# First Gram matrix corrected behind both splits of the second ctx, instead of between them

## Chip, cores and metric

One Trainium2 chip, one of its cores. The metric is the device time of one launch in microseconds (us), the median of several runs.

## The reference, cut to what is computed

Eight batches; x and ctx of a batch are 256 channels (rows) by 1024 columns, all in 32-bit floats.

```python
# cross attention, for each batch b (B=8, C=256, D=1024, 8 groups of 32 channels)
t = Wt @ ctx          # (256, 1024)
p = Wp @ layernorm(x)
g = Wg @ ctx
...
att = sum over a group of (p * g)          # one number per group
y = Wz (per group) @ (att * t)
yn = (y - mean) * rsqrt(var + 1e-5)        # over a group
x = x + tanh(g_xattn) * (yn * gn_w + gn_b + ctx)
# feed-forward with 64 experts of rank 8, for each row
h = layernorm(x); scores = (h Wq^T) keys^T; gate = softmax over the top 16 of 64
x = x + tanh(g_ffn) * 2 * ((h A^T) * gate) B^T
```

## The kernel before, in words

**Tiling.** 256 channels are T = 2 tiles of 128 rows, 1024 columns are NH = 2 halves of 512. A loop over the NB = 8 batches is written out by hand, one program for each engine: SP (SyncE) issues the loads and stores, PE (TensorE) multiplies, DVE (VectorE), ACT (ScalarE) and POOL (GpSimd) work on the elements. Each engine takes its instructions strictly in the order of its program, and each waits on counting semaphores that other engines raise. No scheduler is at work: what stands earlier in the text of an engine's block runs earlier.

**Attention by a Gram matrix.** att needs only M = (normed x) ctx^T, 256 x 256. `whole_gram(0)` (L1104) multiplies the raw x by ctx into two PSUM banks, z_ps[0] and z_ps[1], one for each tile of 128 rows. As x is not yet normed there, `gram_fix(n)` on DVE (L787) subtracts from bank t the row means times the column sums of ctx (`cb_sb`): one instruction of 128 x 256 for each t, which waits for `gram_done` of its bank and raises `M_fixed`. `M_high(n)` on ACT (L545) waits for `M_fixed`, scales by the reciprocal deviation and writes M_first (which lies in zg_sb) for batch 0; it raises `M_hi_s`. `first_n()` on PE (L1198) waits for both and multiplies by Wp. `att_reduce(0)` (L817) on DVE multiplies its result by Wg and sums.

**The group statistics.** `group_means(n)` (L1223, PE) averages the means of u over groups of 32 rows, `group_deviation(n)` (L823, DVE) waits for it (`mean_sum`) and raises `mean_read`, for which `u_variance(n)` (L538, ACT) waits; `group_att_var(0)` (L1229, PE) needs the result.

**Splits in two parts.** The products of u = Wu ctx are done in three passes with each operand split in a high and a low part. Of the second ctx (batch 1), `c_high(t, 1)` on ACT (L520) writes c_hi, and `second_c_low(t)` on DVE (L956) writes c_lo = c_sb - c_hi, 128 x 1024, both operands and the result in SBUF. It waits for c_hi of the tile, for the last u product of batch 0 and for the first low part, and raises `c_lo_s`. `u_product(1)` on PE (L1185) waits for both tiles of c_lo.

**Around it.** On POOL, `x_add(0)` (L418) adds x to ctx of batch 0, four instructions of 128 x 512, all in SBUF. PE's program in this stretch is `ctx_sums(0)`, `whole_gram(0)`, `group_means(0)`, 8 small products for the router (L1342, 64 columns each), `first_n()`, `u_product(1, {0: group_att_var(0)})`, then the transposes `hT(0, 0)` (L1243) of w and the products `z_product(0, 0)` (L1266). ACT's is `c_high(0, 1)`, `c_high(1, 1)`, `u_copy(0)` (L557, four), `M_high(0)`, `u_variance(0)`, the router's high part (L636), then the high parts of twelve lots of weights (L616), then `hT_high(0, 0)` (L574). DVE's goes on with the router's low part (L981), `att_reduce(0)`, and `slopes(0, two_lots)` (L833 to L847), with the low parts of two lots (L744) in it while POOL takes a root (`y_root`, L428); then `first_w` (L855). The four pieces of `first_w` need `xt_done` of `x_add(0)`.

Of the kernel before, what the change touches and what calls it, by code (L numbers as in the profile page):

```python
# [6 lines left out]
def flamingo_block(nc, x, ctx, xT, cT, wt, wzT, wpT, wg, aT, bT, wq, keysT, norms, out):  # L7
# [27 lines left out]
    with ExitStack() as stack:  # L35
# [87 lines left out]
        def gram_bank(n, t):  # L123
            return w_ps[T + t] if n == 2 else z_ps[t]
# [50 lines left out]
        def per_tile(n, t):  # L175
            return T * n + t + 1
# [9 lines left out]
        def per_use(n, k):  # L186
            return USES * n + k + 1
# [543 lines left out]
        def _(dve):  # L731
# [6 lines left out]
            def settle():  # L738
                dve.wait_ge(dve_step, steps[0])
# [41 lines left out]
            def gram_fix(n):  # L781

                dve.wait_ge(cb_s, n + 1)
                settle()
                for t in range(T):
                    dve.wait_ge(gram_done, per_tile(n, t))
                    dve.scalar_tensor_tensor(gram_bank(n, t)[:, 0:C], cb_sb[:, :], neg_x[:, t:t + 1], gram_bank(n, t)[:, 0:C],  # L787
                                             ALU.mult, ALU.add).then_inc(M_fixed, 1)
# [7 lines left out]
            def u_statistics(n, tiles=range(T)):  # L796
                for t in u_tiles(n):
                    if t not in tiles:
                        continue
                    for h in range(NH):  # L800
                        k = NH * t + h
                        dve.wait_ge(u_done, per_use(0, first_uses().index(k)) if n == 0 else u_use(n, k))
                        step(dve.bn_stats(u_st[:, t, 6 * h:6 * h + 6], w_ps[k][:, :]))  # L803
                    settle()
                    instruction = dve.bn_aggr(u_mv[:, t, :], u_st[:, t, :])
                    instruction.then_inc(u_stats, 1)
                    dve.wait_ge(u_stats, u_tile(n, t))
                    dve.tensor_scalar(neg_u[:, t:t + 1], u_mv[:, t, 0:1], -1.0, None, ALU.mult).then_inc(u_mean, 1)  # L808
# [12 lines left out]
            def group_deviation(n):  # L821
                dve.wait_ge(mean_sum, n + 1)
                dve.tensor_tensor(u_dev[:, :], u_mv[:, :, 0], t_ps[1][:, 0:T], ALU.subtract).then_inc(mean_read, 1)  # L823
                if n >= 2:

                    dve.wait_ge(mean_read, n + 1)
                    step(dve.tensor_tensor(a2[:, :], u_dev[:, :], u_dev[:, :], ALU.mult))
                    settle()
                    dve.tensor_tensor(att_var[:, T:2 * T], a2[:, :], u_mv[:, :, 1], ALU.add).then_inc(u_rows, T)
# [122 lines left out]
            def second_c_low(t):  # L952
                dve.wait_ge(c_hi_s, per_tile(1, t))
                dve.wait_ge(u_done, per_use(0, USES - 1))
                dve.wait_ge(first_lo_s, t + 1)
                dve.tensor_tensor(c_lo[:, t, :], c_sb[1][:, t, :], c_hi[:, t, :].bitcast(f32),  # L956
                                  ALU.subtract).then_inc(c_lo_s, 1)
# [16 lines left out]
            minus_means(0)  # L974
            u_statistics(0)
            second_c_low(0)
            gram_fix(0)
            group_deviation(0)
            second_c_low(1)
            dve.wait_ge(router_hi_s, 1)  # L980
            dve.tensor_tensor(A_lo[:, :, NN:ZC], t_ps[0][:, :].rearrange("p (k e) -> p k e", k=KD),  # L981
                              A_hi[:, :, NN:ZC].bitcast(f32), ALU.subtract).then_inc(router_lo_s, 1)
# [476 lines left out]
```

## Time and profile before

| | us |
|---|---|
| median of 3 runs | 324.51 |
| lowest, highest | 324.15, 326.56 |
| the profiled execution | 325.73 |
| its span, first to last instruction | 323.9 |
| PE busy in the span | 319.0 (98%) |
| DVE, ACT, POOL busy | 245.9, 174.9, 168.5 |

The page shows the profiled execution: busy time of each engine, the span in 40 slices with the granted clock of TensorE, the chain of work that ended last, and the costliest groups of instructions. A timeline row gives start, duration, engine, line and operation, with the tensors written and read. Where several instructions are merged (x4), the duration is from the first's start to the last's end. Successive instructions of one engine overlap in the records by some hundredths of a microsecond, since one is started before the last one has drained.

### The profile page before, as it was taken

How to read it: one execution, taken by the hardware profiler on the slowest of the kernel's cores; microseconds unless marked ns; L12 is line 12 of the kernel's file. 1: busy time of each engine (PE TensorE's matmuls, PEld its weight loads, DVE VectorE, ACT ScalarE, POOL GpSimd, SP SyncE). 2: the span in 40 equal slices, each digit the busy share in tenths (PEclk: the TensorE clock that was granted, in tenths of full speed). 3: DMA queues.
4: the chain of work that ended last, by engine and by line, in shares of the span. 5: the costliest groups of instructions: out<-in, count | busy, mean ns of one | idle time of the engine just before them, and what ended most of it. 6: DMA issues, size and time to landing. Idle time of an engine off the chain costs nothing.

```text
span 323.9 us, 5543 instructions
## 1 busy us (share of the span) xinstructions
PE 319.0 (98%) x1960; PEld 290.4 (90%) x1960; DVE 245.9 (76%) x636; ACT 174.9 (54%) x298; POOL 168.5 (52%) x158
## 2 busy tenths in 40 slices
PE   8999999999999999999999999999999999999996
PEld 6688998899988999898999899898999889989985
DVE  1856897596588946888887799788987798789362
ACT  3687845677256485286545658177454654354110
POOL 0464699189463969339581677429591580010000
PEclk9998999999999999999999999999999999999999
DMA  7999900990650585249951899228961631272102
GB/s 248 412 388 397 363 4 7 328 306 10 191 200 13 184 300 190 63 134 272 405 200 34 253 358 361 67 89 275 365 252 61 224 134 74 58 244 82 65 32 99
DMA packets 28091, 62.69 MB, mean 194 GB/s; under 512 B 2448, under 2 KB 12560, under 8 KB 28064
## 3 DMA queue, kind: packets, MB, share of 16 engines
q1 hardware_dynamic: 27712, 62.14, 54.6%
q8 instruction: 16, 0.26, 0.3%
q10 hardware_dynamic: 352, 0.20, 0.2%
q14 instruction: 11, 0.09, 0.1%
HBM read 46.34 MB, written 15.99 MB: 192 GB/s over the span
## 4 chain that ended last, share of the span: by engine, by line
PE 94%; DMA 3%; SPq 1%; issue 0%; ACT 0%; DVE 0%
PE z_ps L1266 20%; PE w_ps L1296 18%; PE w_ps L1185 12%; PE w_ps L1266 12%; PE z_ps L1125 9%; PE w_ps L1303 9%; PE z_ps L1104 4%; DMA cT_first<-in_cT 3%; PE t_ps L1213 2%; PE w_ps L1125 2%; PE t_ps L1243 2%; PE t_ps L1280 1%; PE z_ps L1198 1%; PE z_ps L1213 1%; PE t_ps L1342 1%; PE w_ps L1314 0%
## 5 line engine op out<-in xcount | busy, mean ns | idle before, releaser
L1296 PE MATMUL w_ps<-B_hi,zT_hi 128*128 128x512 f32 x124 | 49.3, 397 | 0.0
L1296 PE MATMUL w_ps<-B_lo,zT_hi 128*128 128x512 f32 x124 | 48.4, 391 | 0.0
L384 POOL TENSOR_TENSOR xT_lo<-xT_in,xT_hi 128x512 fp32r<-128x512 f32 x24 | 30.6, 1298 | 20.5 <-ACT xT_hi L500 17.7
L418 POOL TENSOR_TENSOR c_sb<-c_sb,x_sb 128x512 f32<-128x512 f32 x28 | 36.2, 1329 | 6.9 <-ACT c_sb L603 6.9
L403 POOL TENSOR_TENSOR c_lo<-c_sb,c_hi 128x512 fp32r<-128x512 f32 x24 | 30.3, 1292 | 14.1 <-DVE uw L863 14.1
L557 ACT ACTIVATE uw<-w_ps,neg_u 128x512 f32<-128x512 f32 x32 | 20.2, 686 | 28.8 <-DVE neg_u L808 28.8
L574 ACT ACTIVATE hT_hi<-t_ps 128x512 fp32r<-128x512 f32 x32 | 18.5, 599 | 30.7 <-DVE t_ps L884 22.5
L1266 PE MATMUL z_ps<-A_hi,hT_hi 128*128 128x288 f32 x160 | 34.7, 298 | 0.2 <-ACT hT_hi L574 0.2
L1266 PE MATMUL z_ps<-A_lo,hT_hi 128*128 128x288 f32 x160 | 34.1, 294 | 0.0
L1303 PE MATMUL w_ps<-B_hi,zT_lo 128*128 128x512 f32 x124 | 33.3, 390 | 0.0
L384 POOL TENSOR_TENSOR cT_lo<-cT_in,cT_hi 128x512 fp32r<-128x512 f32 x24 | 30.6, 1300 | 2.4 <-DVE uw L863 2.4
L1303 PEld LDWEIGHTS w_ps<-B_hi,zT_lo 128*128 128x128 f32 x124 | 23.3, 188 | 5.0
L1296 PEld LDWEIGHTS w_ps<-B_hi,zT_hi 128*128 128x128 f32 x124 | 23.3, 188 | 4.4
L1296 PEld LDWEIGHTS w_ps<-B_lo,zT_hi 128*128 128x128 f32 x124 | 23.3, 188 | 4.3
L1266 PEld LDWEIGHTS z_ps<-A_hi,hT_hi 128*128 128x128 f32 x160 | 25.9, 188 | 1.1 <-ACT hT_hi L574 0.4
L1266 PEld LDWEIGHTS z_ps<-A_lo,hT_hi 128*128 128x128 f32 x160 | 25.9, 189 | 0.0
L942 DVE SCALAR_TENSOR_TENSOR uw<-w_ps,tg,uw 128x512 f32<-128x512 f32 x31 | 22.5, 743 | 2.9 <-PE w_ps L1303 2.7
L1266 PE MATMUL z_ps<-A_hi,hT_lo 128*128 128x288 f32 x160 | 24.7, 297 | 0.0
L803 DVE BATCH_NORM_STATS2 u_st<-w_ps 128x6 f32<-128x512 f32 x32 | 21.2, 690 | 3.3 <-PE w_ps L1185 3.3
L1125 PE MATMUL z_ps<-cT_hi,xT_hi 128*128 128x256 f32 x80 | 23.7, 296 | 0.0
L870 DVE TENSOR_TENSOR hT_lo<-t_ps,hT_hi 128x512 fp32r<-128x512 f32 x32 | 21.4, 682 | 1.9 <-ACT hT_hi L574 1.0
L1185 PE MATMUL w_ps<-c_hi,Wu_hi 128*128 128x512 f32 x56 | 22.7, 405 | 0.0
(191 smaller groups left out, 846.8 us busy)
## 6 DMA issues: line engine op xcount, KB each, us to landing
c_sb<-in_ctx SPq DMA_DIRECT2D x16, 512.0 KB, 6.8
x_sb<-in_x SPq DMA_DIRECT2D x16, 512.0 KB, 7.3
xT_in<-in_xT SPq DMA_DIRECT2D x14, 512.0 KB, 6.8
cT_in<-in_cT SPq DMA_DIRECT2D x14, 512.0 KB, 8.1
out_block<-uw SPq DMA_DIRECT2D x14, 512.0 KB, 6.2
w_through<-uw SPq DMA_DIRECT2D x10, 512.0 KB, 3.2
c_sb<-w_through SPq DMA_DIRECT2D x10, 512.0 KB, 4.0
z_through<-zg_sb SPq DMA_DIRECT2D x9, 256.0 KB, 2.3
```

The source lines that it names most:

```text
L384: last = pool.tensor_tensor(lo[:, chunks, :], came[:, chunks, :], hi[:, chunks, :].bitcast(f32), ALU.subtract)
L403: last = pool.tensor_tensor(c_lo[:, t, cols], c_sb[n % 2][:, t, cols], c_hi[:, t, cols].bitcast(f32), ALU.subtract)
L418: last = pool.tensor_tensor(c_sb[n % 2][:, t, cols], c_sb[n % 2][:, t, cols], x_sb[:, t, cols], ALU.add)
L557: act.activation(uw[n % 2][:, t, cols], w_ps[k][:, :], ACT.Identity, bias=neg_u[:, t:t + 1]).then_inc(u_copied, 1)
L803: step(dve.bn_stats(u_st[:, t, 6 * h:6 * h + 6], w_ps[k][:, :]))
L870: dve.tensor_tensor(hT_lo[at], t_ps[g][:, :], hT_hi[at].bitcast(f32), ALU.subtract).then_inc(hT_lo_s, 1)
L942: dve.scalar_tensor_tensor(uw[n % 2][:, t, cols], w_ps[k][:, :], tg2[:, 0:1], uw[n % 2][:, t, cols], ALU.mult, ALU.add).then_inc(out_added, 1)
L1125: last = pe.matmul(gram_bank(n, t)[:, 0:C], a[:, k, t * P:(t + 1) * P], c[:, k, :], start=(k == 0 and a is xT_hi and c is cT_hi), stop=(k ...
L1185: last = pe.matmul(w_ps[k][:, :], w[:, c, rows], v[:, c, cols], start=(c == 0 and w is Wu_hi and v is c_hi), stop=(c == T - 1 and w is Wu_lo))
L1266: last = pe.matmul(banks[i][:, 0:ZH], (hT_lo if low else hT_hi)[:, t, k * P:k * P + P], w[:, k, i * ZH:(i + 1) * ZH], start=(k == 0 and no ...
L1296: pe.matmul(w_ps[k][:, :], zT_hi[:, t, row], w[:, j, cols], start=(j == 0 and w is B_hi), stop=False)
L1303: last = pe.matmul(w_ps[k][:, :], zT_lo[:, t, j * P:(j + 1) * P], B_hi[:, j, cols], start=False, stop=(j == KN - 1))
```

## The change

In DVE's program for batch 0, the second of the two splits, `second_c_low(1)`, stands directly behind the first, and `gram_fix(0)` and `group_deviation(0)` behind both. Nothing is added or removed, and the waits of each piece are the same as before.

```diff
             minus_means(0)
             u_statistics(0)
             second_c_low(0)
+            second_c_low(1)
             gram_fix(0)
             group_deviation(0)
-            second_c_low(1)
             dve.wait_ge(router_hi_s, 1)
```

DVE's order around the place, as the difference of the two programs (L956 is `second_c_low`, L787 `gram_fix` on the banks z_ps, L823 `group_deviation`, L981 the router's low part):

```order
 L808 TENSOR_SCALAR neg_u<-u_mv 128x1
-L956 TENSOR_TENSOR c_lo<-c_sb,c_hi 128x1024
-L787 SCALAR_TENSOR_TENSOR z_ps<-cb_sb,neg_x,z_ps 128x256 x2
-L823 TENSOR_TENSOR u_dev<-u_mv,t_ps 128x2
-L956 TENSOR_TENSOR c_lo<-c_sb,c_hi 128x1024
+L956 TENSOR_TENSOR c_lo<-c_sb,c_hi 128x1024 x2
+L787 SCALAR_TENSOR_TENSOR z_ps<-cb_sb,neg_x,z_ps 128x256 x2
+L823 TENSOR_TENSOR u_dev<-u_mv,t_ps 128x2
 L981 TENSOR_TENSOR A_lo<-t_ps,A_hi 128x8x64
```

The two corrections and the deviation have moved behind one more instruction of 128 x 1024; what follows L981 stands as it did.

ACT's order at the same place, the same in both programs (L557 the copies of u, L545 `M_high(0)`, L538 `u_variance(0)`, L636 and L616 high parts of weights):

```order
L520 ACTIVATE c_hi,c_sum<-c_sb 128x1024 x2
L557 ACTIVATE uw<-w_ps,neg_u 128x512 x4
L545 ACTIVATE zg_sb<-z_ps,x_rs 128x256 x2
L538 ACTIVATE att_var<-u_dev,u_mv 128x1 x2
L636 ACTIVATE A_hi<-t_ps 128x8x64
L616 ACTIVATE A_hi<-A_in 128x512 x8
```

Nothing moved here; L545 waits for L787 of DVE, L538 for L823, and L636 stands behind both. The programs of PE, POOL and SP are also the same in both kernels.

## Rows read from the trace of the kernel before

**Rows 1.** The page, busy time of TensorE in the span: busy us (share), instructions

```profile
PE 319.0 (98%) x1960; PEld 290.4 (90%) x1960; DVE 245.9 (76%) x636; ACT 174.9 (54%) x298; POOL 168.5 (52%) x158
```

**Rows 2.** Chain that ended last, in order of time: start us, us, what

```profile
15.79 5.42 PE z_ps L1104 x24
```

**Rows 3.** Waits of PE from 16 us to the end: us in total, times, longest

```profile
PE z_ps L1104 <- DMA cT_first<-in_cT: 0.3, 1, 0.3
PE z_ps L1266 <- ACT hT_hi L574: 0.2, 1, 0.2
```

**Rows 4.** Timeline of PE: start us, us, line, operation, tensors

```profile
21.25 1.99 PE L1342 MATMUL t_ps<-stage 16*128 16x64 f32 x16
23.17 2.99 PE L1198 MATMUL z_ps<-zg_sb,Wp_in 128*128 128x256 f32 x8
25.60 0.99 PE L1185 MATMUL w_ps<-c_hi,Wu_hi 128*128 128x512 f32 x1
```

**Rows 5.** Timeline of DVE, 18 to 27 us (in brackets: idle before, and what ended it)

```profile
18.22 2.02 DVE L956 TENSOR_TENSOR c_lo<-c_sb,c_hi 128x1024 fp32r<-128x1024 f32 x1 [1.88 <-ACT c_hi L520]
20.16 0.47 DVE L787 SCALAR_TENSOR_TENSOR z_ps<-cb_sb,neg_x,z_ps 128x256 f32<-128x256 f32 x1
21.24 0.49 DVE L787 SCALAR_TENSOR_TENSOR z_ps<-cb_sb,neg_x,z_ps 128x256 f32<-128x256 f32 x1 [0.61 <-PE z_ps L1104]
...
21.71 1.22 DVE L956 TENSOR_TENSOR c_lo<-c_sb,c_hi 128x1024 fp32r<-128x1024 f32 x1
23.91 0.69 DVE L981 TENSOR_TENSOR A_lo<-t_ps,A_hi 128x512 fp32r<-128x512 f32 x1 [0.98 <-ACT A_hi L636]
26.31 0.43 DVE L817 CUSTOM_DVE_ANT_0 z_ps<-z_ps,Wg_sb 128x256 f32<-128x256 f32 x1 [1.71 <-PE z_ps L1198]
```

**Rows 6.** Timeline of ACT, 19 to 33 us

```profile
19.28 0.19 ACT L520 ACTIVATION_READ_ACCUMULATOR c_hi<-c_sb 128x1 f32 x1
19.37 2.41 ACT L557 ACTIVATE uw<-w_ps,neg_u 128x512 f32<-128x512 f32 x4
21.66 0.85 ACT L545 ACTIVATE zg_sb<-z_ps,x_rs 128x256 f32<-128x256 f32 x2
22.37 0.69 ACT L538 ACTIVATE att_var<-u_dev,u_mv 128x1 f32<-128x1 f32 x2
23.28 0.60 ACT L636 ACTIVATE A_hi<-t_ps 128x512 fp32r<-128x512 f32 x1 [0.22 <-PE t_ps L1342]
...
32.98 1.09 ACT L574 ACTIVATE hT_hi<-t_ps 128x512 fp32r<-128x512 f32 x2 [2.87 <-PE t_ps L1243]
```

**Rows 7.** Timeline of POOL, third and fourth piece of x_add(0)

```profile
17.88 1.27 POOL L418 TENSOR_TENSOR c_sb<-c_sb,x_sb 128x512 f32<-128x512 f32 x1
19.11 2.25 POOL L418 TENSOR_TENSOR c_sb<-c_sb,x_sb 128x512 f32<-128x512 f32 x1
```

**Rows 8.** Timeline of DVE and POOL where both work in SBUF, 29 and 35 us

```profile
29.06 1.28 DVE L744 TENSOR_TENSOR A_lo<-A_in,A_hi 128x512 fp32r<-128x512 f32 x2
29.22 1.09 POOL L428 TENSOR_TENSOR y_rs<-y_ve,minus_half 128x2 f32<-128x2 f32 x1 [2.23 <-DVE y_ve L841]
...
35.48 1.41 DVE L744 TENSOR_TENSOR A_lo<-A_in,A_hi 128x512 fp32r<-128x512 f32 x1
36.30 1.75 POOL L391 TENSOR_TENSOR A_lo<-A_in,A_hi 128x512 fp32r<-128x512 f32 x1
```

**Rows 9.** All eight of L428: duration ns min/median/max, first and last start

```profile
L428 POOL TENSOR_TENSOR y_rs<-y_ve,minus_half x8: 688/690/1088, 29.2 to 281.4; 128x2 f32<-128x2 f32 x8
```

**Rows 10.** Timeline of DVE and ACT, the same correction and scaling of batch 1

```profile
55.05 0.87 DVE L787 SCALAR_TENSOR_TENSOR z_ps<-cb_sb,neg_x,z_ps 128x256 f32<-128x256 f32 x2
55.62 0.84 ACT L545 ACTIVATE M_hi<-z_ps,x_rs 128x256 fp32r<-128x256 f32 x2 [2.01 <-DVE z_ps L787]
```

**Rows 11.** Windows of PE: A:B, us, busy (x), granted clock, DMA share, GB/s

```profile
24.00:27.40 3.40, 3.40 (x10) 0.50 1.06 395
27.40:32.40 5.00, 5.00 (x25) 1.00 1.04 398
```

## The prediction

> **What bounds the kernel now.** I read the page's busy times first. TensorE is busy for 319.0 of 323.9 us [rows 1], so only something that makes PE wait, run slower or do less can move the end; the other engines count where PE waits for them. Next I read the chain that ended last: from 15.79 us, where the first Gram matrix starts, it lies on PE nearly without a break [rows 2]. The waits of PE say the same: from 16 us to the end it is shown idle twice, 0.3 us for the first transposed inputs and 0.2 us for a high part of the turned w [rows 3]. The change lies behind the first and ahead of the second. It gives PE no work and takes none, so with no stall to remove on PE, a gain could only come from TensorE's clock. The question is whether the later correction makes PE wait, and how long.
>
> PE's row of work there is: 16 small router products, start 21.25; then `first_n`, start 23.17; then `u_product(1)`, start 25.60 [rows 4]. `first_n` needs both tiles of M_high, which need both corrections.
>
> **Slack before the change.** The two corrections start at 20.16 and 21.24, the second only then because its Gram bank was not ready (0.61 us idle), and it ends at 21.73 [rows 5]. ACT scales both tiles in 21.66 to 22.51 [rows 6]. PE comes to `first_n` at 23.17, so M is there 0.66 us early (0.56 with the handover that is worked out below) [rows 4, 6]. The other consumer, `u_product(1)`, has its second low part at 21.71 + 1.22 = 22.93 and starts at 25.60 [rows 4, 5]: 2.67 us of slack. Having that low part sooner brings nothing; that half of the move is worth 0.
>
> **When the second split now ends.** Its inputs are ready: c_hi of tile 1 is complete at 19.28 + 0.19 = 19.47, and the first split hands over to the next instruction at 20.16 [rows 5, 6]. So it is issued at 20.16. How long it takes depends on POOL. The first split took 2.02 us and the second 1.22, at the same shape [rows 5]. Beside the first, POOL's third piece of `x_add` ran 17.88 to 19.15 unstretched, while the fourth, started at 19.11, took 2.25 instead of 1.27 and ended at 21.36 [rows 7]. That reads as one at a time: the split waits from 18.22 to 19.15 and works 1.09 us, until 20.24; the fourth piece waits for it and works 1.12 us behind it. A second place agrees: L744 takes 1.41 us against 0.68 for one of a pair (1.28 for two, which overlap by 0.08), and the POOL instruction that starts at 36.30 behind it takes 1.75 [rows 8]. The Trainium skill, "GPSIMD Engine Reference", Key points, says that GpSimd shares its SBUF interfaces with VectorE and that the two contend when a VectorE instruction has two SBUF inputs. This trace agrees (2.02 against 1.22 us); without that rule the move would look free, as the third case below works out.
>
> Before, the correction stood at 20.16, which has its bank in PSUM and only one large input in SBUF: it took 0.47 us beside POOL, its usual time [rows 5, 7], while the second split at 21.71 came after POOL had finished. Now the second split meets POOL's fourth piece, which has waited since 19.11. Who goes first? The nearest row is the root at 29.22. It came while a pair of L744 ran from 29.06 to 30.34. The root took 1.09 us against a median of 0.69 [rows 8, 9], so it was held 0.40 us, to 29.62, about the end of the first of the pair (29.06 + 0.68 = 29.74), and ended at 30.31, ahead of the pair's end. A POOL instruction that waits thus gets its turn between two back-to-back DVE instructions. I take that: the fourth piece runs to 21.36 as before, then the split works 1.09 us, to 22.45, and hands over 0.08 us before its end, at 22.37. The bounds: DVE keeps its turn (issue 20.16, 1.22 us, handover at 21.30), or the two are interleaved as on average in the first split (2.02 us, handover at 22.10), or POOL's piece goes first (22.37).
>
> **From the split to PE.** Both Gram banks are full by 21.24, so the corrections follow back to back. Batch 1 shows such a chain: corrections start at 55.05, the scaling on ACT starts 0.57 us later and takes 0.84 for both tiles [rows 10], 1.41 from the first correction's start to the last scaling's end. So 22.37 + 1.41 = 23.78. From ACT to PE I add 0.10 us, an estimate from the handover from DVE to ACT (the reader starts 0.57 us behind a correction that takes 0.47 [rows 5, 10]): 23.88. Against 23.17 that is a **stall of 0.71 us on PE**, at a place where it now has none.
>
> **What else is late, and what covers it.** `group_deviation` moves from about 21.7 to 22.37 + 0.87 = about 23.2, and ACT issues `u_variance` behind the scaling at about 23.7 instead of 22.37; it takes 0.69 [rows 6, 10]. The router's high part behind it starts at about 24.35 instead of 23.28, and the twelve lots with it, 1.07 us late. ACT is idle for 2.87 us ahead of 32.98 [rows 6], which covers this. The router's low part on DVE is then at 23.91 + 1.07 = 24.98 to 25.67, ahead of `att_reduce` at 26.31 + 0.71 [rows 5]. POOL takes up the first lots later by the same 1.07 us, and its next root is 0.71 us later too; the two instructions of 1.3 us in front of it have 2.23 us of idle time behind them [rows 8]. So these cost 0. If this cover were gone, the 1.07 us would cost its excess over the stall, 0.36 us. SP's queue and all DMAs stand untouched.
>
> After `first_n`, `att_reduce`, `slopes`, the first w and the turned h hang on its result and shift with PE. The wait of 0.2 us for hT_hi [rows 3] is made by the same chain, so it does not absorb the shift, and no wait for a transfer lies behind it.
>
> **Sum.** 0 (work) + 0.71 (stall) - 0 (low part sooner) = +0.71 us. The profiled execution took 325.73 us, 1.83 more than its span of 323.9, and would be 326.4; it lay 1.22 above the median, 324.51. From the median: 324.51 + 0.71 = **325.2 us**, 0.2% slower. Three runs of this kernel spread by 0.7% (324.15 to 326.56), so within 1%, about 3.2 us, is what a measurement can hardly tell from no change.
>
> **TensorE's clock.** From 24.00 to 27.40 PE was granted 0.50, the 1.2 GHz level, and from 27.40 again 1.00, the 2.4 GHz level [rows 11]. Ahead of the fall PE did the small router products and started `first_n`. The 3.4 us at half speed cost 1.7 us against full speed. The stall falls just ahead of this stretch and adds 0.71 us without products to a time of small products. If the stretch keeps its length, nothing changes. The Trainium skill, "TensorE: Matmul & The Clock Gate", Part 1, says that the clock gate follows how busy the array has lately been. That speaks for a longer slow stretch and not a shorter one; no row here shows by how much.
>
> **The rivals.**
> 1. *PE stalls by POOL's turn, clock as before* (the forecast): +0.71, 325.2 us. Chance 0.48.
> 2. *The stall is smaller.* Interleaved, the handover at 22.10 gives 22.10 + 1.51 = 23.61 and a stall of 0.44: 324.95 us. Speaks for it: the 2.02 us are also what equal shares would give; against it: the third piece at 1.27 was not stretched. Chance 0.12.
> 3. *No stall.* DVE keeps its turn: handover at 21.30, ACT is busy with the copies of u until 21.78 and then scales from 21.87 to 22.71, with the handover 22.81, 0.36 us ahead of 23.17. The change then does nothing to the time: 324.5 us. Against it stands the root at 29.22. Chance 0.20.
> 4. *The slow stretch grows.* A second stretch as long as the first costs 1.7 us: 324.51 + 0.71 + 1.7 = 326.9 us. For it: PE has less to do just ahead of a fall. Against it: full-width products follow at once. Chance 0.10.
> 5. *The slow stretch shrinks or goes.* Then up to 1.7 us come back: 325.2 - 1.7 = 323.5 us. For it: part of the time that was slow is now idle; against it: nothing here makes PE busier. Chance 0.07.
> 6. *Slower beyond 1%.* The place is the same; the idle time makes TensorE fall back to 1.2 GHz several times. The price is 1.7 us for each stretch of 3.4 us, so it decides from two further stretches on: 0.71 + 3.4 = 4.11, 328.6 us. Against it: from 27.40 PE has full-width products without a gap and runs at 1.00. Chance 0.03.
>
> **How the numbers follow.** Cases 1 to 3 lie between 324.5 and 325.2 and hold 0.80; the spread of the median itself adds some 0.4 us below and more above, since one of three runs lay 2 us higher. The range 323.9 to 326.7 takes these in, and leaves out most of cases 4 to 6. Cases 1 to 5 are all within 1%. Slower by over 1% is case 6; faster by over 1% has no mechanism, as even case 5 gives 0.3%, and gets 0.01. That leaves 0.96 for no change.
>
> **What would show it.** In the timeline of DVE the second split should start at about 20.16 and take 2.0 to 2.3 us, with POOL's fourth piece ending near 21.36 (near 22.5 if DVE keeps its turn). The corrections should stand at 22.3 to 23.2, M_high should end at about 23.8, `first_n` start at about 23.9, and a new wait of PE on ACT's L545 should be shown at `first_n`, 0.4 to 0.7 us. The granted clock should be 0.50 for about 3.4 us around 24 to 28. The forecast is wrong if PE starts `first_n` at 23.2 all the same, if ACT is idle for less than about 1 us ahead of hT_hi, or if the slow stretch has another length.

## The result, and the profile after

| | before | changed |
|---|---|---|
| median of 20 runs each, us | 324.65 | 326.70 |
| lowest, highest | 324.07, 326.56 | 324.72, 327.24 |
| the profiled execution | 325.73 | 326.67 |
| its span | 323.9 | 324.8 |

The ratio of the times is 1.0035, 95% interval 1.0019 to 1.0051: 0.35% slower, within the 1% called no change, clear of zero. A second series of the same kernel (e5 below) gave 1.0051 (1.0032 to 1.0070).

The medians differ by more (2.05 us) than the ratio says, because the times of both kernels lie in two clusters. Which one a run belongs to shows in its mean granted clock: near 1.00, or 0.995. The profiled run of before is of the second kind and holds one stretch of 3.4 us at the 1.2 GHz level [rows 11]; half speed for 3.4 of 324 us is what a mean of 0.995 comes to, so I take the other runs at 0.995 to hold one as well. For these 20 runs of before only the times are on record, and they are sorted by them: 11 lie up to 324.67, 9 from 325.79 on. So before had 9 of 20 runs with such a stretch, the changed kernel 13 of 20, and the middle run fell into the other cluster. Like with like:

| median us (number of runs) | mean clock near 1.00 | mean clock 0.994 or 0.995 |
|---|---|---|
| before | 324.42 (11) | 326.17 (9) |
| changed | 325.12 (7) | 326.76 (13) |
| difference | +0.70 | +0.59 |
| before, beside e5 | 324.29 (21) | 325.75 (8) |
| changed again, e5 | 325.34 (5) | 326.85 (7) |
| difference | +1.05 | +1.10 |

In each of the two series every full-clock run of the changed kernel (324.72 or more, 325.18 or more) took longer than every one of before (324.67 or less, 324.56 or less), so in these the difference within the cluster is clear of noise. In the series of e1 to e4, however, 7 of the 17 full-clock runs of before took 325.14 to 325.45 and the other ten 324.06 to 324.63: a spread of the size of the effect that the clock does not explain, and whose cause is open.

Two profiled executions with one half-speed stretch each, before and after, differ by 0.94 us.

The waits of PE from 16 us to the end, in the changed kernel (us in total, times, longest):

```profile
PE z_ps L1198 <- ACT zg_sb L545: 1.0, 1, 1.0
PE z_ps L1266 <- ACT hT_hi L574: 0.2, 1, 0.2
```

The first is new: `first_n` waits for M_high, which [rows 3] did not have. The second is the same wait as in [rows 3]; it neither grew nor absorbed anything. The timeline of DVE in the changed kernel, both splits and what follows them, with the second split by itself:

```profile
18.11 4.51 DVE L956 TENSOR_TENSOR c_lo<-c_sb,c_hi 128x1024 fp32r<-128x1024 f32 x2 [1.89 <-ACT c_hi L520]
...
20.33 2.29 DVE L956 TENSOR_TENSOR c_lo<-c_sb,c_hi 128x1024 fp32r<-128x1024 f32 x1
...
22.54 0.87 DVE L787 SCALAR_TENSOR_TENSOR z_ps<-cb_sb,neg_x,z_ps 128x256 f32<-128x256 f32 x2
```

Two splits take 4.51 us, where before they took 2.02 and 1.22 [rows 5]. The second was issued at 20.33 and took 2.29 us; the corrections that started at 20.16 and 21.24 in [rows 5] now start at 22.54. POOL's fourth piece of `x_add` in the changed kernel:

```profile
19.28 2.25 POOL L418 TENSOR_TENSOR c_sb<-c_sb,x_sb 128x512 f32<-128x512 f32 x1
```

It takes 2.25 us, as in [rows 7], and ends at 21.53; the second split ends 1.09 us behind it, at 22.62. Then ACT and PE in the changed kernel:

```profile
23.11 0.84 ACT L545 ACTIVATE zg_sb<-z_ps,x_rs 128x256 f32<-128x256 f32 x2 [1.45 <-DVE z_ps L787]
23.84 0.66 ACT L538 ACTIVATE att_var<-u_dev,u_mv 128x1 f32<-128x1 f32 x2
24.40 0.59 ACT L636 ACTIVATE A_hi<-t_ps 128x512 fp32r<-128x512 f32 x1
...
33.83 1.09 ACT L574 ACTIVATE hT_hi<-t_ps 128x512 fp32r<-128x512 f32 x2 [2.60 <-PE t_ps L1243]
```

```profile
24.10 3.53 PE L1198 MATMUL z_ps<-zg_sb,Wp_in 128*128 128x256 f32 x8 [0.96 <-ACT zg_sb L545]
```

ACT was busy with copies when the corrections ended before [rows 6]; now it is idle for 1.45 us and waits for them. `first_n` starts at 24.10 after 0.96 us of idle time, against 23.17 [rows 4]. ACT's later queue had cover: it is still idle for 2.60 us ahead of hT_hi (2.87 in [rows 6]), and hT_hi moved from 32.98 to 33.83, by 0.85 us. The span grew by 0.9.

The granted clock of the changed kernel's profiled run over the stretches of [rows 11]:

```profile
24.00:27.40 3.40, 3.30 (x9) 0.52 1.06 394
27.40:32.40 5.00, 5.00 (x25) 1.00 1.04 395
```

One half-speed stretch, about as long as before and at the same place. As far as these two executions go, the clock took next to no part in the 0.94 us.

### The profile page after: what moved, and what is told of

Its sections match the earlier page's. It is cut to its first block, busy times and chain, and to the rows that moved or that the text cites. A ratio compares the mean times of both kernels' runs of the same rounds, so it can differ in the third digit from the quotient of the medians.

```text
span 324.8 us, 5543 instructions
## 1 busy us (share of the span) xinstructions
PE 318.9 (98%) x1960; PEld 290.3 (89%) x1960; DVE 247.2 (76%) x636; ACT 175.0 (54%) x298; POOL 168.5 (52%) x158
## 4 chain that ended last, share of the span: by engine, by line
PE 91%; DMA 3%; SPq 1%; issue 1%; DVE 1%; ACT 1%; ACTq 0%; DVEq 0%
PE z_ps L1266 20%; PE w_ps L1296 18%; PE w_ps L1185 12%; PE w_ps L1266 12%; PE z_ps L1125 9%; PE w_ps L1303 9%; DMA c_sb<-in_ctx 3%; PE t_ps L1213 2%; PE z_ps L1104 2%; PE w_ps L1125 2%; PE t_ps L1243 2%; PE z_ps L1198 1%; PE t_ps L1280 1%; PE z_ps L1213 1%; DVE c_lo L956 1%
## 5 line engine op out<-in xcount | busy, mean ns | idle before, releaser
L557 ACT ACTIVATE uw<-w_ps,neg_u 128x512 f32<-128x512 f32 x32 | 20.2, 686 | 28.8 <-DVE neg_u L808 28.8
L1125 PE MATMUL z_ps<-cT_lo,xT_hi 128*128 128x256 f32 x80 | 22.6, 283 | 0.0
```

The costliest lines, as they stand in the source:

```text
L557: act.activation(uw[n % 2][:, t, cols], w_ps[k][:, :], ACT.Identity, bias=neg_u[:, t:t + 1]).then_inc(u_copied, 1)
L1125: last = pe.matmul(gram_bank(n, t)[:, 0:C], a[:, k, t * P:(t + 1) * P], c[:, k, :], start=(k == 0 and a is xT_hi and c is cT_hi), stop=(k ...
```

## Experiments

The first theory: DVE and POOL take turns at SBUF, instruction by instruction; POOL's piece goes ahead of the second split, the corrections come late, and PE stalls for it. The rivals: the order alone does it; ACT's queue behind the deviation carries part; and, for the times, TensorE's clock. Each ratio below is to runs of the kernel before on the same chip. There are three such series: e1 to e4, e5 to e7, and e8 to e11.

**e1: POOL's piece held back.** In `x_add`, to the changed kernel:

```diff
-                    for cols in pieces():
+                    for i, cols in enumerate(pieces()):
+                        if n == 0 and t == T - 1 and i == NH - 1:
+                            pool.wait_ge(c_lo_s, T)
```

> The changed kernel, with POOL's fourth piece of x_add(0) held back until both low parts of the second ctx are written. Theory (one of DVE and POOL at a time; the piece goes first and makes the second split late): the second split starts near 20.3 and takes about 1.2 us, the corrections start near 21.45, M_high ends near 22.9, PE waits less than 0.1 us at first_n, and the time goes back to that of the kernel before within 0.1 us (ratio 1.000; 0.9980 to 0.9985 of the changed kernel in like clock states). Rival (the order alone makes the correction late, POOL's piece is beside the point): the corrections start no sooner than about 22.2 and PE still waits 0.5 us or more, ratio 1.002.

Ratio 1.0009 (0.9986 to 1.0031), no different from before. Timeline of DVE in e1, then of POOL:

```profile
18.67 3.30 DVE L958 TENSOR_TENSOR c_lo<-c_sb,c_hi 128x1024 fp32r<-128x1024 f32 x2 [1.94 <-ACT c_hi L522]
21.89 0.87 DVE L789 SCALAR_TENSOR_TENSOR z_ps<-cb_sb,neg_x,z_ps 128x256 f32<-128x256 f32 x2
```

```profile
22.05 1.27 POOL L420 TENSOR_TENSOR c_sb<-c_sb,x_sb 128x512 f32<-128x512 f32 x1 [2.29 <-DVE c_lo L958]
```

Both splits together take 3.30 us instead of 4.51, POOL's piece alone 1.27 instead of 2.25, and the only wait of PE shown behind 16 us is the 0.2 us for hT_hi. This execution is shifted by 0.56 us against the changed kernel from its first split on (18.67 against 18.11), so the corrections come at 21.89 and not 21.45; against the start of the first split they come 3.22 us later instead of 4.43. The order of the splits is the changed one here. Without the meeting of the second split and POOL's piece it costs little or nothing: at full clock 324.57 against 324.58 beside it, with a half-speed stretch 325.95 against 326.06. Against the lower ten of the full-clock runs of before alone (median 324.27) 0.3 us would remain, which no wait in the trace accounts for. What this run does not show is a clock like that of before: 6 of 10 runs had the stretch, against 4 of 21 of before beside them, though there was no stall.

**e2: only the deviation moved.** To the kernel before:

```diff
             gram_fix(0)
-            group_deviation(0)
             second_c_low(1)
+            group_deviation(0)
```

> The kernel before, with only group_deviation moved behind the second split, gram_fix between the splits as before. Theory (the correction alone carries the cost): group_deviation at about 22.85, u_variance about 0.5 us later on ACT, the router's high part about 0.4 us later, PE without a wait at first_n, ratio to before 1.000. Rival (the deviation and ACT's queue behind it carry part of it): PE waits somewhere between 23 and 34 us, 0.3 us or more, ratio 1.001 or above.

Ratio 0.9997 (0.9976 to 1.0017). Timeline of DVE in e2, the deviation and the router's low part:

```profile
22.82 0.15 DVE L823 TENSOR_TENSOR u_dev<-u_mv,t_ps 128x2 f32<-128x2 f32 x1
24.18 0.69 DVE L981 TENSOR_TENSOR A_lo<-t_ps,A_hi 128x512 fp32r<-128x512 f32 x1 [1.21 <-ACT A_hi L636]
```

The deviation started at 22.82 instead of 21.64, the router's low part at 24.18 instead of 23.91, and PE had no wait at `first_n`. So the late deviation carries none of the cost. ACT's queue is pushed back by 0.3 us only here, against 1.1 us in the changed kernel (24.40 against 23.28); that the 1.1 us cost nothing rests on the changed kernel's own trace, where 2.60 us of idle time are left ahead of hT_hi and PE's wait for it is still 0.2 us.

**e3: the dose.** The changed kernel with the low part of tile 1 computed twice:

```diff
+                if t == T - 1:
+                    step(dve.tensor_tensor(c_lo[:, t, :], c_sb[1][:, t, :], c_hi[:, t, :].bitcast(f32),
+                                           ALU.subtract))
+                    settle()
```

> The changed kernel, with the low part of tile 1 computed twice (the same values), each behind the other. Theory (what DVE does ahead of the correction comes one for one on PE): the corrections start about 1.2 us later, near 23.75, PE's wait at first_n grows from 0.96 to about 2.2 us, and the time by 1.2 us over the changed kernel in the same clock state: 326.4 with the clock full throughout, 328.0 with one slow stretch; over before 1.9 us in either state, ratio 1.006 or, if slow stretches become the rule, up to 1.010. Rival (part of the stall falls in the slow stretch and is half price): 0.6 us over the changed kernel in like states.

Ratio 1.0097 (1.0074 to 1.0121). Waits of PE in e3:

```profile
PE z_ps L1202 <- ACT zg_sb L545: 2.2, 1, 2.2
```

The wait grew from 1.0 to 2.2 us, as the theory has it. None of the four timed runs was at full clock: three have the mean clock of one usual stretch (median 328.15), and one of a stretch about twice as long (329.16). The three against 326.76 to 326.85 of the changed kernel in the other series: +1.3 to 1.4 us for 1.2 us of added wait; against 326.06 of before in its own series, +2.1 us for a wait of 2.2. The stall is paid in full; the rival of half price falls. The profiled run, with a span of 327.4 us, is the one with the longer stretch:

```profile
24.00:30.60 6.60, 4.68 (x11) 0.50 1.04 395
```

**e7: the piece halved.** POOL's fourth piece of 512 columns is cut in two of 256, in the changed kernel:

```diff
-                    for cols in pieces():
+                    small = [slice(0, HALF), slice(HALF, HALF + HALF // 2), slice(HALF + HALF // 2, D)]
+                    for cols in small if n == 0 and t == T - 1 else pieces():
```

> The changed kernel, with POOL's fourth piece of x_add(0) cut in two of 256 columns. Theory (DVE and POOL take turns by instruction, each waiting for one of the other's): the first half runs ahead of the second split, about 0.65 us, the split then works 1.1 us, the second half runs behind it; the split ends near 22.0 by the clock of the changed kernel's trace, 0.5 to 0.6 us sooner, and the wait at first_n falls from 0.96 to 0.35 to 0.45 us; 0.5 us less than the changed kernel at like clock. Rival (DVE waits until POOL has nothing left to do, or POOL's whole queue goes first): the split ends no sooner than before and the wait stays at 0.9 to 1.1 us. Second rival (they share the path in small grains): the split takes about 2.0 us with the piece halved or not.

Timeline of POOL and DVE in e7, the two halves and the second split:

```profile
19.44 1.72 POOL L419 TENSOR_TENSOR c_sb<-c_sb,x_sb 128x256 f32<-128x256 f32 x1
20.49 1.75 DVE L957 TENSOR_TENSOR c_lo<-c_sb,c_hi 128x1024 fp32r<-128x1024 f32 x1
21.13 1.70 POOL L419 TENSOR_TENSOR c_sb<-c_sb,x_sb 128x256 f32<-128x256 f32 x1
```

The first half waits for the first split, works and ends at 21.16. The second split then works 1.08 us, to 22.24, and the second half ends 0.59 us behind it, at 22.83. The split took 1.75 us instead of 2.29. Each waits for one instruction of the other, at both lengths tried. Both rivals fall: POOL's whole queue did not go first, and fine-grained sharing would have left the split's length alone. The wait of PE at `first_n` in e7:

```profile
PE z_ps L1199 <- ACT zg_sb L546: 0.2, 1, 0.2
```

It fell by 0.8 us, more than the 0.5 to 0.6 expected. Half of that is the halved piece (the split ended 0.38 us sooner, at 22.24 instead of 22.62); the rest is that PE came to `first_n` 0.4 us later in this execution (23.54 instead of 23.14). The time was 324.86 (ratio 1.0006, 0.9986 to 1.0026), with 8 of 10 runs at full clock, and there 324.75 against 325.34 of the changed kernel in the same series: 0.6 us less.

### The clock

The remaining question was whether the change also makes the half-speed stretch more frequent. Counted by mean clock (0.995 or less is a run with at least one such stretch):

| series | before | runs with a half-speed stretch |
|---|---|---|
| first | 9 of 20 | changed 13 of 20 |
| e1 to e4 | 4 of 21 | e1 6 of 10, e2 3 of 10, e3 (wait of 2.2 us) 4 of 4, e4 2 of 6 |
| e5 to e7 | 8 of 29 | changed (e5) 7 of 12, e6 (stall filled) 0 of 12, e7 2 of 10 |
| e8 to e11 | 13 of 29 | e8 3 of 12, e10 3 of 12, e11 5 of 12 |
| all | 34 of 99 | changed 20 of 32 |

**e5: the changed kernel again.**

> The changed kernel as it is, once more beside the kernel before, to count runs by their mean clock. Theory (the stall costs its own length in either clock state, and besides makes a slow stretch likelier): 0.65 to 0.9 us more than before in like clock states, and more than half of the runs at a mean clock of 0.995, against a third of the runs of before. Rival (the clock has nothing to do with the change, 13 of 20 against 9 of 20 was chance): equal shares within 2 in 10, and a ratio of 1.002.

7 of 12 against 8 of 29 before beside it. Together 20 of 32 against 34 of 99: shares this far apart arise by chance less than once in a hundred (Fisher's exact test, 0.007). That pools series in which before itself goes from 4 of 21 to 13 of 29. Each series against its own runs of before, the two taken together, gives 0.04, and neither alone would do (0.34 and 0.08). So the change probably makes the stretch more frequent; it is not beyond doubt. The cost at full clock was 1.05 us, above the 0.9 expected. The wait of PE in this profile of the same kernel:

```profile
PE z_ps L1198 <- ACT zg_sb L545: 0.6, 1, 0.6
```

The corrections came at nearly the same time (22.49 against 22.54), but PE reached `first_n` 0.3 us later (23.42 against 23.14): how POOL and PE stand to each other in an execution sets the length of the stall.

**e6: the stall filled.** To the changed kernel, ahead of `first_n`:

```diff
             last.then_inc(router_done, 1)
+            pe.wait_ge(u_copied, u_use(0, USES - 1))
+            keep_busy(8)
             first_n()
```

> The changed kernel, with eight 128x128 transposes of the identity on PE between the router products and first_n, written to a bank that is overwritten later; they take the place of the stall (0.9 us). Theory (the idle time makes the slow stretch likelier): no wait at first_n over 0.2 us, the same time as the changed kernel at full clock, 325.1 us, but slow runs only as often as before, a third to a half. Rival (the slow stretch comes from something else, or from the small products ahead): slow runs as often as in the changed kernel, about two in three or more.

No run of 12 had the stretch, fewer than the third to a half that I expected. Median 325.09 us, as at full clock without the filler; ratio to before 1.0017 (1.0003 to 1.0031), against 1.0051 for the unfilled kernel on the same chip in the same series. Windows of PE in e6 at the place:

```profile
24.00:27.40 3.40, 3.40 (x19) 1.00 1.06 396
```

So 0.9 us of transposes in the place of the idle time save the half-speed stretch (0 of 12 against 7 of 12 unfilled, 0.005 by the same test) and cost nothing. This version clearly beats the changed kernel of the same series, as e7 does with its 1.0006, and is the only one without a single stretch. Neither beats the kernel before.

**e4: the router row broken up.** To the kernel before, cut to PE's order (`second_u_high` does the passes of the first two banks that need c_hi alone, `second_u_rest` the others, with one or two router products after each tile; the router's parts on ACT and DVE stand later):

```diff
             group_means(0)
-            pe.wait_ge(wq_in, 16)
-            pe.wait_ge(keys_in, 16)
-            for k in range(KD):
...
-            first_n()
-            u_product(1, {0: lambda: group_att_var(0)})
+            second_u_high()
+            first_n()
+            second_u_rest({0: lambda: group_att_var(0)})
```

> The kernel before with PE's order changed: the small router products no longer stand in a row ahead of first_n, but two or one at a time between the products of u_product(1); ahead of first_n PE does the passes of its first two banks that need c_hi alone. Router's high and low part stand later on ACT and DVE. Theory (the row of small products is what TensorE's fall to 1.2 GHz follows): the granted clock stays 1.00 from 20 to 33 us in nearly every run, mean clock near 1.000, and the time is that of the fast cluster of the kernel before, 324.4 us, in every run; mean 0.8 us less than before, ratio 0.997 to 0.999. Rival (the fall comes regardless of what PE does there, for instance by a clock of its own): half of the runs still show a mean clock of 0.995 and 326.2 us, ratio 1.000. If the latency chain behind first_n were the bound, both clusters move up by some tenths.

A miss: ratio 1.0078 (1.0035 to 1.012, without the slowest run, 331.62). Four runs at full clock had a median of 326.71, and two had a much longer half-speed stretch (mean clock 0.984). In the profiled run, one of these two, PE waited 0.8 us for hT_hi. Windows of PE in e4:

```profile
25.00:28.90 3.90, 3.90 (x19) 1.00 1.05 395
29.00:38.70 9.70, 9.70 (x31) 0.50 0.99 386
```

Breaking up the row did not remove the stretch; where it came, it was later and lasted longer, with PE busy throughout. A whole row of small products is thus not needed for a fall; small ones still stood between the large.

**e8, e10: work of full width in the row, kernel before.** e8 moves two products of u_product(1) between the router's k = 3 and k = 4 (`early_pair`; they are left out of `u_product` later), e10 adds four transposes there:

```diff
                                  start=True, stop=True)
+                if k == KH - 1:
+                    early_pair()
...
+                if k == KH - 1:
+                    pe.wait_ge(u_copied, u_use(0, USES - 1))
+                    keep_busy(4)
```

> The kernel before, with two of u_product(1)'s own products (512 columns, those of the first bank and tile 0 that need c_hi alone) moved into the middle of the router row. PE's work is the same; first_n starts 0.45 us later. Theory (a long light stretch ahead of first_n makes the slow stretch likely; work of full width in it prevents it): at most 1 run in 10 with a mean clock of 0.995, against about a third of before, and at full clock 324.3 to 324.6 us, since w of the first tile was ready about 0.3 us ahead of its transposes; mean 0.3 to 0.5 us less than before, ratio 0.999. Rival (only transposes or an absent stall matter): a third of the runs slow, ratio 1.000.

> The kernel before, with four 128x128 transposes of the identity in the middle of the router row (0.46 us of added work on PE). Theory: no or nearly no slow runs, and at full clock 0.45 us more than before, 324.75; ratio about 1.000 in the mean of all runs. Rival (the transposes of the filled stall worked only because they filled a stall): a third of the runs slow, both clusters 0.45 us up, ratio 1.0014.

3 of 12 runs in each had the stretch, against 13 of 29 of before beside them. That is too few to tell from before, and far from none, so both theories failed. At full clock e8 took 325.03 and e10 325.06, against 324.38 before: both cost 0.65 to 0.7 us. For e8, with no work added, I had expected 0.3 at most. Its PE runs the same 7.5 us from the start of `first_n` (24.04) to the first transposes of w (31.55) as e2 (23.21, 30.76), although it has two products fewer to do in between. `att_reduce` ends at 27.05 in e8, 3.01 us behind the start of `first_n` as in e2, and `group_att_var(0)` on PE starts right behind it, at 27.11. So what is behind `first_n` hangs on `first_n`'s start, and work done ahead of it does not come back.

**e11: the stall filled with later work.** To the changed kernel, with the same kind of exception in `u_product` as in e8:

```diff
             last.then_inc(router_done, 1)
+            early_passes()
             first_n()
```

> The changed kernel, with four of u_product(1)'s own products (0.9 us, c_hi only, first bank) moved ahead of first_n, where the stall was. Theory: no wait at first_n over 0.2 us, hardly a slow run; at full clock the time lies between before and the filled stall: PE has done 0.9 us of later work, but the chain from first_n over att, slope and w to the turned h starts as late as in the changed kernel, so 0.3 us at most come back: 324.8 us, with a new wait of PE at its first transposes of w (L1243) of 0.3 to 0.6 us. Rival (the stall's cost is PE's lost time alone): all 0.9 us come back, 324.3 us.

Ratio 1.0024 (1.0001 to 1.0047); at full clock 325.30, 0.9 more than before beside it. The changed kernel was not run in this series, and cost 0.70 and 1.05 in the others, so nothing that can be measured came back. PE's wait moved. Waits of PE in e11:

```profile
PE t_ps L1243 <- DVE att_var L817: 0.6, 1, 0.6
```

L1243 there is `group_att_var(0)`, not the transposes where I expected the wait. It stands behind the first bank of `u_product`, and waits for `att_reduce`. With four of that bank's six products done in advance there is too little left to cover the reduction. Five of 12 runs had the half-speed stretch, though `first_n` no longer waited and PE had full-width products in the stall's place; I had expected hardly any.

## Why the prediction was right, and where it was not

- **What bounds, and the direction:** right. PE without a stall there before, one wait after, and the span longer by about its length. e3 shows the slope: 1.2 us more wait, 1.3 to 1.4 us more time.
- **The turn of POOL's piece:** right, and the step that decided. Expected about 2.3 us for the second split, measured 2.29. The root at 29.22 [rows 8] was a sound witness of the order, but not of the price: the pair of L744 beside it took 1.28 us, two times 0.68 less the overlap, so the second of the pair was not held by the root. That a turn of POOL holds DVE for a whole instruction came from the first split and from 35.48. e1 and e7 show that it is the cause and that the turn goes by instruction.
- **From the split to PE:** right in kind, 0.25 us short. Corrections 22.37 expected, 22.54 measured: POOL's pieces started 0.17 us later in that execution (15.59 against 15.42), and that goes through to the end of the split. From ACT's end (23.95) to PE's start (24.10) it took 0.15, not 0.10. And PE was ready for `first_n` 0.03 us sooner (24.10 less 0.96 is 23.14, against 23.17). So the stall was 0.96, not 0.71. The second profile of the same kernel (e5) shows 0.6 us, so the expected value lies within the spread between executions.
- **Steps costed at 0:** right. e2 shows it for the deviation. For ACT's queue, 1.1 us late as expected, the changed kernel's trace shows it: 2.60 us of idle time left ahead of the high part of h.
- **The sum:** +0.71 expected. Like with like, 0.59 to 1.10 were measured, and 0.94 between the two profiles. The time lies in the range, but at its edge (326.7), since the other term was missing from the sum; that it lies in it at all is owed to the range's allowance for the spread of the median, made for one slow run of three. The size of the shift in the median, 2.05 us, is in part luck: had 9 of the changed kernel's 20 runs held the stretch and not 13, the median would have been at most about 325.5.
- **The clock:** this step failed. "If the stretch keeps its length, nothing changes" took the half-speed stretch for a fixed part of every run. It is in about a third of the runs of before. The two profiled executions have it at equal length, as the step says, but the runs do not. Three runs at 324.15, 324.51 and 326.56, with a profile at 325.73 that held such a stretch, could have said so. The term that belonged in the sum is a share times a price: (20/32 - 34/99) x 1.6 us = 0.45 us. With the stall of 0.6 to 1.1 it gives 1.0 to 1.6 us, and the ratios of 1.0035 and 1.0051 are 1.1 and 1.7 us. The rival of a second stretch (326.9) was close to the measured median for the wrong reason: no second stretch, but one stretch in more of the runs. That the idle time is what raises the share is not shown. For it speak e6 (0 of 12 with transposes in its place), e7 (2 of 10 with 0.2 us of it) and e3 (4 of 4 with more of it). Against it speak e1 (6 of 10 without a stall, against 4 of 21 of before beside it) and e11 (5 of 12 with full-width products in its place). What decides in the kernel before, where PE is not idle there and the clock falls all the same, stays open too: e4, e8 and e10 did not find it.

## What to carry to other kernels

Before swapping two instructions of one engine, look at what the other engine is doing in SBUF at the new time: here a VectorE instruction with two SBUF inputs waited out GpSimd's running one, so the same work cost 1.2 us in one place and 2.3 in another, and halving GpSimd's piece cut that wait from 1.20 to 0.67 us. Ask what latency chain hangs on the result that is pushed back; filling the stall with later work gave nothing back here (e11), since the chain was as long as the work beside it. When runs fall in clusters, compare within a cluster and count the clusters, since a median can jump from one to the other.

## What the runs showed of the hardware

- In the traces above, DVE instructions with two SBUF inputs and POOL's pieces took turns by whole instruction: a DVE split of 128 x 1024 that takes 1.22 us alone took 2.29 behind a POOL piece of 512 columns and 1.75 behind one of 256. Two DVE splits issued back to back did not keep POOL's fourth piece out: issued at 19.28, it ended at 21.53, and the second split, issued at 20.33, worked behind it. The correction, with its bank in PSUM, was not held beside the same piece (0.47 us [rows 5]).
- TensorE's half-speed stretch comes in some runs of the same kernel and not in others, and the program has a part in how often: 34 of 99 runs before, 20 of 32 of the changed kernel, 0 of 12 with eight transposes in the stall's place. It lasted 3.4 us in the profiled runs of before and after, and cost about 1.6 us; in e3 it lasted over 6.6 us and in e4 over 9.7 us, there with PE busy throughout. The Trainium skill, "TensorE: Matmul & The Clock Gate", Part 1, has the gate follow how busy the array has been; e6 fits that, while by PE's busy share alone the stretches of before (3.40 of 3.40 us busy, and no wait ahead of it [rows 3, 11]) and of e4 could not be told.
